# Where six groups of transposes stand in the order of a fused attention and mixture-of-experts kernel

## The reference

```python
xn = layernorm(x)
y = xn @ U                                     # U is 128 x 32
attn = softmax(-|y_t - y_j|^2) @ xn            # per block, 512 x 512
shared = silu(xn @ sg) * (xn @ su) @ sd        # sg, su 128 x 1024
probs = softmax(rmsnorm(xn) @ router_w.T)      # 8 experts, top 2, rw normalised
for e in range(8):                             # 320 tokens at most per expert
    xg = xn[dispatch[e]]
    routed[dispatch[e]] += rw * ((silu(xg @ rg[e]) * (xg @ ru[e])) @ rd[e])   # inner width 512
out = x + attn + shared + routed
```

## Time and profile before

| | value |
|---|---|
| median of 3 runs | 158.18 us (158.13 to 158.49) |
| profiled execution | 158.14 us, span 156.7 us |
| PE busy | 151.4 us, 97% of the span |
| DVE busy | 118.9 us, 76% |
| ACT busy | 103.7 us, 66% |
| POOL busy | 81.3 us, 52% |
| mean granted clock of PE | 0.998 of full speed |
| the chain that ended last | PE 91%, DVE 5%, DMA 1% |

### The profile page before, as it was taken

One profiled execution on the slowest core, in us unless ns is written; L12 is line 12 of the kernel. 1 busy time (PEld: TensorE's weight loads), 2 busy tenths in 40 slices (PEclk: granted clock), 3 DMA queues, 4 the chain that ended last, 5 costly groups with the idle time before them and its releaser, 6 DMA issues.

```text
span 156.7 us, 3107 instructions
## 1 busy us (share of the span) xinstructions
PE 151.4 (97%) x964; PEld 134.9 (86%) x964; DVE 118.9 (76%) x294; ACT 103.7 (66%) x217; POOL 81.3 (52%) x98
## 2 busy tenths in 40 slices
PE   6899999999999999999999999999999999999992
PEld 6867765999999988888878999999999999878991
DVE  4899959999834699999997676786786786546861
ACT  3359999989588397867756669899687566344200
POOL 7550400447777778778500003698988857454000
PEclk9999999999999999999999999999999999999999
DMA  3999999991111116527059400414232111019486
GB/s 114 254 297 113 169 285 340 346 304 60 51 55 58 60 33 199 166 84 198 0 114 298 139 0 2 149 32 126 59 105 67 34 46 33 25 35 280 95 273 191
DMA packets 26350, 20.72 MB, mean 132 GB/s; under 512 B 2301, under 2 KB 22296, under 8 KB 26336
## 3 DMA queue, kind: packets, MB, share of 16 engines
q1 hardware_dynamic: 24544, 17.89, 44.1%
q0 software_dynamic: 1792, 2.65, 5.6%
HBM read 12.36 MB, written 7.92 MB: 129 GB/s over the span
## 4 chain that ended last, share of the span: by engine, by line
PE 91%; DVE 5%; DMA 1%; issue 0%; SPq 0%; ACT 0%; DVEq 0%
PE bank L1158 16%; PE bank L1159 16%; PE bank L1160 16%; PE bank L1306 9%; PE bank L1239 9%; PE bank L1359 5%; PE bank L1361 5%; PE bank L1360 5%; PE bank L1224 2%; PE bank L1375 2%; DVE stats L839 2%; PE bank L1386 2%; DMA acc<-in_L_attn_x_dram 1%; PE bank L1177 1%; PE bank L1207 1%; DVE lgT L927 0%
## 5 line engine op out<-in xcount | busy, mean ns | idle before, releaser
L658 ACT ACTIVATE silu<-bank 128x512 f32<-128x512 f32 (+1 forms) x64 | 33.1, 520 | 29.4 <-PE bank L1160 29.2
L552 POOL DMA_INDIRECT slots_dram<-row,slot_i x32 | 34.0, 1064 | 11.2 <-issue 9.4
L985 DVE TENSOR_TENSOR bank<-bank,silu 128x320 f32<-128x320 f32 (+1 forms) x48 | 27.1, 565 | 15.5 <-ACT silu L658 12.6
L571 POOL DMA_INDIRECT routed_dram<-eo,xg x24 | 23.0, 958 | 11.5 <-DVE eo L1025 6.3
L991 DVE TENSOR_TENSOR hid_lo<-bank,hid_hi 128x320 fp32r<-128x320 f32 (+1 forms) x48 | 26.2, 547 | 0.0
L1158 PE MATMUL bank<-xnT_hi,sw_hi 128*128 128x512 f32 x62 | 25.3, 409 | 0.1
L1159 PE MATMUL bank<-xnT_lo,sw_hi 128*128 128x512 f32 x62 | 24.5, 396 | 0.0
L1160 PE MATMUL bank<-xnT_hi,sw_lo 128*128 128x512 f32 x62 | 24.4, 394 | 0.0
L666 ACT CAST hid_hi<-bank 128x320 fp32r<-128x320 f32 (+1 forms) x48 | 22.9, 477 | 0.0
L559 POOL TENSOR_TENSOR ew_lo<-sw_raw,ew_hi 128x1024 fp32r<-128x1024 f32 x3 | 7.2, 2413 | 19.4 <-ACT ew_hi L682 19.4
L1306 PEld LDWEIGHTS bank<-sd,hid_s 128*128 128x128 f32 x128 | 14.8, 192 | 1.0 <-issue 0.9
(11 more groups left out here) (186 smaller groups left out, 313.2 us busy)
## 6 DMA issues: line engine op xcount, KB each, us to landing
sw_raw<-in_L_ffn_rg_dram SPq DMA_DIRECT2D x8, 256.0 KB, 3.1
sw_raw<-in_L_ffn_ru_dram SPq DMA_DIRECT2D x8, 256.0 KB, 3.5
rd_raw<-in_L_ffn_rd_dram SPq DMA_DIRECT2D x8, 256.0 KB, 3.4
routed_dram<-fill SPq DMA_DIRECT2D x1, 2048.0 KB, 12.6
routed<-routed_dram SPq DMA_DIRECT2D x8, 256.0 KB, 4.2
slots_dram<-fill SPq DMA_DIRECT2D x1, 1300.0 KB, 13.6
xg<-slots_dram SPq DMA_DIRECT2D x8, 130.0 KB, 2.2
row<-row SPq DMA_DIRECT2D x1, 1024.0 KB, 8.1
```

The lines of the kernel that those rows point to most:

```text
L552: G.indirect_dma_start(slots_dram, bass.IndirectOffsetOnAxis(slot_i[:, k, t:t + 1], 0), row[:, t, 0:RW], None, bounds_check=E * CAP - 1, o ...
L571: G.indirect_dma_start(routed_dram, bass.IndirectOffsetOnAxis(xg[0:n, e % XB, r, 1:2].bitcast(I32), 0), eo[0:n, e % 2, r, :], None, bounds ...
L658: C.activation(silu[:, q % 2, 0:n], gate_bank(q)[:, 0:n], ACT.Silu).then_inc(silu_ready, 1)
L985: V.tensor_tensor(hid, up[:, 0:n], silu[:, q % 2, 0:n], ALU.mult).then_inc(hid_ready, 1)
```

## The change

Two helpers are added. In a step that holds `turn_slots` (`beside_slots`), the job of the step before is turned; in the step before such a step nothing is turned. This applies to `turn_out` on PE and to `block_sum` and `expert_out` on DVE. Block 2 is turned in step 28 instead of 27, expert e (0 to 4) in step 32 + 4e instead of 31 + 4e: six jobs. On PE, `turn_out` stands right in front of `turn_slots`, so 7 transposes (block 2) or 6 (the experts) follow one another. Block 1 (step 19) and experts 5 (step 51), 6 (step 55) and 7 (step 57) stay. `copy_out` on ACT stays for all jobs. No instruction is added or removed.

```diff
@@ -92,6 +92,17 @@
+    def beside_slots(step):
+
+        kind, i, c = ORDER[step]
+        return kind == "expert" and c == 0 and i + 1 < E
+
+    def turned_after(step):
+
+        if beside_slots(step):
+            return job_after(step - 1)
+        return None if beside_slots(step + 1) else job_after(step)
@@ -1108,8 +1119,8 @@
                 if q == CLOSE:
                     expert_out(E - 1)
-                elif job_after(q) is not None:
-                    of, n = JOBS[job_after(q)]
+                elif q < CLOSE and turned_after(q) is not None:
+                    of, n = JOBS[turned_after(q)]
                     if of == "block":
                         block_sum(n)
                     else:
@@ -1444,8 +1455,8 @@
                 if q == CLOSE:
                     turn_out(len(JOBS) - 1)
-                elif job_after(q) is not None:
-                    turn_out(job_after(q))
+                elif q < CLOSE and turned_after(q) is not None:
+                    turn_out(turned_after(q))
                 if (kind, i, c) == ("block", EARLY - 1, 5):
                     turn_slots(0)
                 elif kind == "expert" and c == 0 and i + 1 < E:
```

## The result

The changed kernel took 159.36 us (median of 6 runs, 159.14 to 160.09) against 158.18 us (158.09 to 158.49): ratio 1.0083, interval 1.0065 to 1.0102. It is slower by 1.2 us; the forecast was 158.3 and the range ended at 158.85. The profiled execution took 159.54 us, with a span of 158.1.

What follows compares the result with a forecast made beforehand. PE was taken to bound the kernel from step 8 to the end. Profiled 158.14 + 0 (merged runs) + 0.16 (slots of expert 7) = 158.30, 0.04 under the median, so 158.34, stated as 158.3; range 157.95 to 158.85.

Steps and rivals of the forecast that it cites:

- Merged runs gain 0: PE's six merged runs of transposes: entering or leaving a run costs nothing; 0 to 0.06 us over six, taken as 0.
- the rival with a price of changing over: On PE, changing between transposes and products has a price, six of which are saved: 0.50 us faster, 157.64; chance 0.05.
- The first write on POOL 1.31 later, and POOL passes it on whole: POOL's queue, without slack, keeps the 1.31 us delay of expert 0's output for all writes and splits of experts 0 to 4.
- Down weights of expert 7: ACT's cast at 117.27, room 0.09, no stall: Load ahead of the last slots: ACT casts at 117.27, DVE's product is done at 119.19, PE needs it at 119.28; cost 0.
- The last slots land 2.3 us after their issue, PE waits 0.16: Expert 7's slots, before the last slot turn, land at 123.27 and PE loads at 123.29, 0.16 us late; chance 0.55.
- The room of 1.17 us: In the kernel before, expert 7's slots land at 121.96 and PE loads them at 123.13; less than the 1.31 delay.
- The bounds: Limits for PE's wait for the last slots: 0 if they land 0.16 earlier, 0.76 us if landing takes 2.9.
- clearly late: Rival: the last slots take 2.9 us to land, not 2.3, and PE stands still 0.76 us: 158.90; chance 0.12.

Runs made afterwards that it cites:

- h2: Changed kernel with only the turn of expert 0 moved, the other five as in the kernel before: 159.25 us, ratio 1.0054 to the kernel before.
- h4: Kernel before, no turn moved, with 1.1 us of needless POOL work in front of the first write: 159.51 us, ratio 1.0080.
- i1: Changed kernel with all 60 warm-up products written out (loop body of 60 instead of 5): 158.99 us, ratio 1.0061 to the kernel before.
- i2: Kernel before with all 60 warm-up products written out (loop body of 60 instead of 5): 158.08 us, ratio 1.0012.
- h1: The changed kernel as it is, run again on the chip of h2 and h4: 159.61 us, ratio 1.0092 to the kernel before.
- g1: Changed kernel with 6 slot buffers instead of 5: 158.41 us, ratio 1.0030 to the kernel before.

## Why the prediction was wrong

- *Merged runs gain 0.* Right: 0.80 us for six transposes and a product against 0.81; 23.71 against 23.70 us over four experts. The same rows refute the rival with a price of changing over. They don't fit the 56 ns either that the Trainium skill, page "TensorE: Matmul & The Clock Gate", section "Back-to-back issue gap", gives for an isolated product of 128 columns: in the merged runs, too, a transpose costs 0.11 us.
- *The first write on POOL 1.31 later, and POOL passes it on whole.* Right: 1.31 in relation to PE (1.44 by the clock of the span, 101.32 less 99.88), and from the first write to the last issue 19.8 us in both kernels (119.66 - 99.88 and 121.13 - 101.32). h2 and h4 show that this delay brings the loss with one turn moved or none.
- *Down weights of expert 7: ACT's cast at 117.27, room 0.09, no stall.* Right in the changed kernel (117.35); i1 showed the stall that comes when this load is later by 0.4.
- *The last slots land 2.3 us after their issue, PE waits 0.16.* This is the step that failed. It measured 3.4 us and 1.06 (PEld 1.29), and 1.2 us of PE's time. The chain and the place were right; the term that was sized wrongly is the landing of the last slots. I took 2.3 from the one row with nothing queued behind the load, and held that all traffic beside it moves along with it. The instruction fetch does not: it goes, by and large, with the place in PE's program and not with POOL's queue. With 110 more instructions of PE in front it came at 111.7 (i1, i2) and not near 122; but in two profiles of the same changed kernel it lay 1.1 and 3.7 us ahead of where slot turn 7 was due (122.32 and 119.68). The room of 1.17 us in the kernel before would also have covered that fetch in any link of the chain, and the change spent all of it. With a room of about zero, 1 us of fetch in any link (last write 3.2 for 2.1, or load 3.4 for 2.3) becomes 1 us of PE.
- *The bounds.* The upper one, 0.76, came from the slowest small load in the trace (2.9), at a place where another load stood behind it. The trace before did hold a larger figure, which I did not look for: the write issued at 120.83, in the stretch of the earlier trace rows, took 3.2 us to land, and the fetch at 122.0 lay in its way. A load or write struck by a fetch was never priced, and the rival "clearly late" got 0.12 where a fetch that began 0.05 us behind the old landing should have made it the likeliest. Its own size, 0.76, was too small as well, so this is not a right rival with a low chance.

What stays open: h1 has 0.36 us more than h2 in its median and not in its profile, and the turns of experts 1 and 2 were never moved by themselves. Why the loads of the routed rows end later in i1 and g1, and why the place of the fetch differs between profiles of one kernel, was not looked into; only one profile was taken of each run.

## What to carry to other kernels

A wait that is nearly used up is not free: count the room in front of each load that a moved step pushes, and compare it with the longest disturbance that can hit any link of its chain, not with the delay alone. A queue with next to no idle time between its instructions (POOL here, for 28 us) passes a delay of its first instruction on to all that wait for its last. When a new order only makes equal work adjacent, measure from the trace whether a run of 4 costs more per piece than a run of 3 before expecting a gain.

## What the runs showed of the hardware

**An instruction fetch delays the transfers beside it.** The 16 KB packets took 0.88 to 1.6 us each; a load or write in whose way one fell landed 0.7 to 1.2 us later (3.4 for 2.3, 3.2 and 3.3 for 2.1, and 2.8 for 2.1). That they belong to PE is read from i1 and i2, where a longer program of PE moved them. The Trainium skill, page "Runtime: NRT & Kernel Launch", section "Instruction fetch mechanics", says that instructions are refilled in blocks of 16 KiB by a DMA queue of the sequencer's own and that the cost of a boundary is "mostly hidden". The size agrees with the trace. For PE itself the cost was hidden on the chips without the pause (with a fetch at 102.2 it took 5.93 us from slot turn 3 to 4, as for the next expert), but not for the transfers beside it.

**A subtraction on DVE with both operands in SBUF stood still while POOL subtracted in SBUF.** The one of 128x512 took 0.68 us alone and 3.06 us beside a subtraction on POOL of 2.41 us, which was not lengthened (2.41 and 2.42). The Trainium skill, page "SBUF — State Buffer", section "SBUF: two separate sides", calls the port pair that the two share an exclusive lock: whichever starts first gets it, and the other blocks for the whole instruction. The trace agrees on the blocking. By the recorded starts it was DVE that came first, by 0.09 us (103.26 and 103.35), and DVE that blocked. In the kernel before, DVE instructions that read one operand from PSUM show no such lengthening: beside POOL's subtraction from 111.97 to 114.40 those at 112.88 and 113.29 took 0.50 and 0.48 us, as elsewhere.
